# Ten zero products in place of fourteen, a last tile normalised on VectorE, and a new order on every engine

## The chip, the cores and the metric

One NeuronCore of one Trainium2 chip runs the whole kernel. The metric is the device time of one execution in microseconds (us); lower is better. The engines are named as the profile names them: PE (TensorE), DVE (VectorE), ACT (ScalarE), POOL (GpSimd) and SP (SyncE, which here only issues DMAs).

## The reference

`x` is 8 sequences of 512 rows of 256 numbers. A layer of attention with a decaying memory is followed by a gated feed-forward layer on numbers rounded to FP4, each with a layer norm behind it:

```python
# attention: chunked scan, equal to a decaying causal product
v = x @ W_write.T
reads[t] = sum over s < t of gamma**(t-1-s) * (x[t] . x[s-1]) * v[s]      # x[-1] = 0, gamma = sigmoid(decay)
x = layernorm(2 * x + exp(log_alpha) * reads @ W_read.T)
# feed-forward: q(.) rounds blocks of 16 numbers to the FP4 grid with a scale of max|.|/6
h = silu(q(x) @ q(w_gate).T) * (q(x) @ q(w_up).T)                          # 704 wide
x = layernorm(x + q(h) @ q(w_down).T)
```

## The kernel before

Everything stays in SBUF; only the inputs and the output go through HBM. A sequence n is cut into four tiles of 128 rows (k = 4n + t is a tile's number, 0 to 31). fp32 operands are split into a rounded part (`_hi`) and a remainder (`_lo`), and each product is made of three: hi with hi, hi with lo, lo with hi. ACT mostly makes the `_hi` copy, DVE or POOL the remainder.

On PE, for a sequence n: `scores(n, j)` makes row block j of the score matrix (512 - 128j columns, 6 products) and DVE's `decay_scores` multiplies it with the decay mask (`pr`, counted by `pr_ready`); `values(n, u)` multiplies two tiles with the combined weights W_write and W_read (12 products of 256 columns; `v_lo_ready`); `reads(n, u)` multiplies scores and values (9 products for u = 0, 21 for u = 1) and DVE's `x_residual` takes it from PSUM (`z_ready`). The layer norm and the rounding to FP4 go over ACT, DVE and POOL, then `xq_transpose(n, u)` turns two tiles round (4 transposes; `xqT_lo_ready`). For each tile k follow `gate_up(k, b, t, half)` (12 products of 512 columns for half 0, 6 of 384 for half 1), SiLU on ACT, `hidden` on DVE, the rounding of h, `h_transpose(k, t, g)` (4 and 2 transposes; `hT_lo_ready`), `down(k, t)` (17 products of 256 columns) and DVE's `out_residual` (`o_ready`). The layer norm of the output: ACT squares (`out_deviations`), DVE makes -mean and variance (`out_moments`, 128x1), POOL the power -0.5 and then shift = -mean * rstd (`out_rstd`, L417 and L419), ACT the tile itself (`out_layernorm`, L713), and SP stores it.

The weights are combined and rounded at the start by the same engines: `combine` makes W_write.T W_read.T in PSUM, DVE's `scale_comb` multiplies it with alpha, ACT rounds it, DVE's `rest_comb` makes `comb_lo`. `w_maxima` to `w_dequant` round the six blocks of the feed-forward weights, `w_transpose(f)` and `w_subtract(f)` turn them round on PE (`wT_lo_ready`).

Each engine's program is one list of such calls, written out by hand for the start (sequences 0 to 2 or so) and the end, with a loop `body(b)` between for b = 2, 3 and 4 (k = 4b, n = b + 1), which is unrolled. Engines work their list in order and wait on semaphores. PSUM has eight banks of 512 columns: `gu[0]` to `gu[3]` and `bank[0]` to `bank[3]`; several kinds of result share a bank, so most PE calls carry a second wait (`free`, the list in brackets), until DVE or ACT has taken out what the bank held before. Ahead of its real work PE multiplies zeros (L1825), 14 times 512 columns:

```python
pe.wait_ge(zeros_ready, 1)
for _ in range(14):
    nc.tensor.matmul(gu[:, 3, :], zeros[:, 0:P], zeros[:], start=True, stop=True)
```

The loads are issued by SP in the order first half of x transposed (ACT issues the second), weights 0, attention weights, weights 1, x transposed of sequence 1, weights 2, x of sequence 0, weights 3 to 5; later loads wait for the buffer.

Of the kernel before, what the change touches and what calls it, by code (L numbers as in the profile page):

```python
# [37 lines left out]
P = 128  # L38
# [14 lines left out]
def mk_seq_postln_kernel(nc, x_rows, xt_rows, w_attn, w_ffn, scalars, out):  # L53
# [18 lines left out]
    with ExitStack() as ctx:  # L72
# [93 lines left out]
        w_bank = (gu[:, 3, :], bank[0], bank[3], gu[:, 2, :], gu[:, 1, :], gu[:, 0, :], gu[:, 3, :], bank[3], bank[2])  # L166
# [33 lines left out]
        hT_filled, hT_hi_ready, hT_lo_ready = sem("hT_filled"), sem("hT_hi_ready"), sem("hT_lo_ready")  # L200
        down_filled, o_ready, o_dev, o_var, o_rstd_ready, o_shift_ready, out_ready = (
# [52 lines left out]
        def _(sp):  # L254
# [54 lines left out]
            store(11, 3)  # L309
            load_x(7)  # L310
            store(12, 0)
# [18 lines left out]
            store(31, 3)  # L330
# [5 lines left out]
        def _(pool):  # L336
# [89 lines left out]
            p_rest(0, 1)  # L426
            w_dequant(0)
            p_rest(0, 2)
            p_rest(0, 3)
            w_normalise(2)  # L430
            w_dequant(1)
            x_rstd(0, 0)
            p_rest(1, 0)
            p_rest(1, 1)
            w_dequant(2)
            w_normalise(3)
            p_rest(1, 2)
# [1633 lines left out]
```

## Time and profile before

| | us |
|---|---|
| median of 3 runs | 326.65 (326.39 to 327.18) |
| the profiled execution | 326.19 |
| its span, first to last instruction | 324.5 |

A row of a timeline gives the start and the duration in us from the span's start, the engine, the line, the instruction with what it writes and reads, how many were merged (x2), and in brackets how long the engine had been idle before it and what ended that. Durations of PE rows overlap, since products are pipelined: the next starts before the one before has ended.

### The profile page before, as it was taken

How to read it: one execution, taken by the hardware profiler on the slowest of the kernel's cores; microseconds unless marked ns; L12 is line 12 of the kernel's file. 1: busy time of each engine (PE TensorE's matmuls, PEld its weight loads, DVE VectorE, ACT ScalarE, POOL GpSimd, SP SyncE). 2: the span in 40 equal slices, each digit the busy share in tenths (PEclk: the TensorE clock that was granted, in tenths of full speed). 3: DMA queues.
4: the chain of work that ended last, by engine and by line, in shares of the span. 5: the costliest groups of instructions: out<-in, count | busy, mean ns of one | idle time of the engine just before them, and what ended most of it. 6: DMA issues, size and time to landing. Idle time of an engine off the chain costs nothing.

```text
span 324.5 us, 6515 instructions
## 1 busy us (share of the span) xinstructions
PE 314.7 (97%) x2065; PEld 285.2 (88%) x2065; DVE 293.5 (90%) x754; ACT 210.8 (65%) x516; POOL 239.9 (74%) x257
## 2 busy tenths in 40 slices
PE   8999999999999999999999999999999999999993
PEld 3899888979988999899999999899989889999983
DVE  4999898999898999698996989999999999999982
ACT  7378977594915786348926687466657745665774
POOL 1869859857975789956996688687677767569672
PEclk9999999999999999999999999999999999999999
DMA  6821300210010202020010200020000000001002
GB/s 230 295 67 67 128 3 0 68 66 2 1 65 18 82 2 75 24 81 20 32 68 16 83 1 33 2 81 17 18 2 33 18 0 33 19 16 34 33 31 69
DMA packets 8242, 15.69 MB, mean 48 GB/s; under 512 B 1040, under 2 KB 5136, under 8 KB 8208
## 3 DMA queue, kind: packets, MB, share of 16 engines
q1 hardware_dynamic: 7920, 15.01, 13.5%
q8 instruction: 17, 0.28, 0.4%
q10 hardware_dynamic: 288, 0.26, 0.3%
q14 instruction: 17, 0.14, 0.1%
HBM read 11.08 MB, written 4.19 MB: 47 GB/s over the span
## 4 chain that ended last, share of the span: by engine, by line
PE 70%; DVE 18%; issue 6%; ACT 4%; POOL 1%; DVEq 0%; POOLq 0%; ACTq 0%
PE gu L1690 11%; PE gu L1694 11%; PE gu L1691 11%; PE bank L1690 5%; PE bank L1691 5%; PE bank L1694 5%; PE bank L1778 4%; DVE h_y L1071 3%; PE bank L1700 2%; PE bank L1703 2%; PE bank L1704 2%; DVE w_raw L1182 2%; PE bank L1752 2%; PE gu L1825 2%; DVE hqT_lo L1209 2%
## 5 line engine op out<-in xcount | busy, mean ns | idle before, releaser
L410 POOL TENSOR_TENSOR h_q<-h_g,h_ns 128x704 f32<-128x704 f32 x32 | 47.3, 1477 | 39.5 <-DVE h_g L1076 36.0
L1690 PE MATMUL gu<-guT_hi,xqT_hi 128*128 128x512 f32 (+1 forms) x192 | 74.9, 390 | 0.5 <-DVE w_raw L1182 0.5
L1691 PE MATMUL gu<-guT_lo,xqT_hi 128*128 128x512 f32 (+1 forms) x192 | 72.1, 376 | 0.0
L681 ACT ACTIVATE w_raw<-gu 128x512 f32<-128x512 f32 x64 | 29.3, 461 | 47.2 <-PE gu L1694 46.8
L1694 PE MATMUL gu<-guT_hi,xqT_lo 128*128 128x512 f32 (+1 forms) x192 | 56.7, 377 | 0.5 <-DVE xqT_lo L1173 0.5
L403 POOL TENSOR_TENSOR h_n<-w_raw,h_rs 128x704 f32<-128x704 f32 x32 | 49.0, 1531 | 9.3 <-DVE h_rs L1066 8.8
L1690 PEld LDWEIGHTS gu<-guT_hi,xqT_hi 128*128 128x128 f32 x192 | 36.1, 188 | 6.7 <-issue 1.3
L1694 PEld LDWEIGHTS gu<-guT_hi,xqT_lo 128*128 128x128 f32 x192 | 35.6, 188 | 6.7 <-DVE xqT_lo L1173 0.9
L1691 PEld LDWEIGHTS gu<-guT_lo,xqT_hi 128*128 128x128 f32 x192 | 36.2, 188 | 5.2
L1071 DVE SCALAR_TENSOR_TENSOR h_y<-h_sq,h_n 128x704 f32<-128x704 bf16 x34 | 36.3, 1069 | 1.6 <-ACT h_sq L685 1.5
L1182 DVE TENSOR_TENSOR w_raw<-w_raw,gu 128x512 f32<-128x512 f32 x64 | 32.3, 506 | 2.9 <-ACT w_raw L681 2.2
L365 POOL TENSOR_TENSOR pr_lo<-pr,pr_hi 128x512 fp32r<-128x512 f32 (+3 forms) x32 | 29.1, 917 | 3.6 <-ACT pr_hi L645 3.6
L1076 DVE SCALAR_TENSOR_TENSOR h_g<-h_sq,h_y 128x704 f32<-128x704 bf16 x34 | 31.4, 924 | 0.2
L1209 DVE TENSOR_TENSOR hqT_lo<-bank,hqT_hi 128x512 fp32r<-128x512 f32 (+1 forms) x48 | 28.1, 590 | 2.5 <-ACT hqT_hi L701 2.5
L685 ACT ACTIVATE h_sq<-h_n 128x704 bf16<-128x704 f32 x32 | 25.3, 789 | 6.3 <-POOL h_n L403 6.3
L1690 PE MATMUL bank<-dnT_hi,hqT_hi 128*128 128x256 f32 x120 | 29.2, 279 | 0.0
L1691 PE MATMUL bank<-dnT_lo,hqT_hi 128*128 128x256 f32 x120 | 29.2, 279 | 0.0
L417 POOL TENSOR_TENSOR o_rstd<-o_ve,neg_half 128x1 f32<-128x1 f32 x32 | 23.4, 731 | 7.1 <-DVE o_ve L1225 7.1
L701 ACT CAST hqT_hi<-bank 128x512 fp32r<-128x512 f32 (+1 forms) x48 | 24.0, 508 | 7.1 <-PE bank L1778 7.0
L1188 DVE TENSOR_REDUCE h_am<-w_raw 128x44 f32<-128x704 f32 x32 | 27.9, 873 | 0.2
L713 ACT ACTIVATE wq_gu<-wq_gu,o_shift,o_rstd 128x256 f32<-128x256 f32 x32 | 19.1, 598 | 12.0 <-POOL o_shift L419 11.9
L395 POOL TENSOR_TENSOR x_q<-x_g,x_ns 128x512 f32<-128x512 f32 x16 | 18.7, 1167 | 9.0 <-DVE x_g L1076 9.0
(156 smaller groups left out, 941.1 us busy)
## 6 DMA issues: line engine op xcount, KB each, us to landing
xs<-in_x_rows_dram SPq DMA_DIRECT2D x8, 512.0 KB, 3.3
out_dram<-wq_gu SPq DMA_DIRECT2D x32, 128.0 KB, 1.7
x_full<-in_xt_rows_dram SPq DMA_DIRECT2D x7, 512.0 KB, 3.3
w_raw<-in_w_ffn_dram SPq DMA_DIRECT2D x6, 352.0 KB, 5.9
w_pair<-in_w_attn_dram SPq DMA_DIRECT2D x1, 512.0 KB, 5.1
x_full<-in_xt_rows_dram SPq DMA_DIRECT2D x1, 256.0 KB, 2.8
x_full<-in_xt_rows_dram ACTq DMA_DIRECT2D x1, 256.0 KB, 3.4
scal<-in_scalars_dram ACTq DMA_DIRECT2D x1, 1.0 KB, 1.7
```

Of the source, the lines that this page charges most:

```text
L365: nc.gpsimd.tensor_tensor(pr_lo[:, c], pr[:, c], pr_hi[:, c].bitcast(F32), ALU.subtract).then_inc(pr_lo_ready, 1)
L403: nc.gpsimd.tensor_tensor(blocks(h_n[:, p, :]), blocks(h[:, p, :]), per_block(h_rs[:, p, :], HB), ALU.mult).then_inc(h_norm, 1)
L410: nc.gpsimd.tensor_tensor(blocks(h_q[:, p, 0:I]), blocks(h_g[:, p, :]), per_block(h_ns[:, p, :], HB), ALU.mult).then_inc(h_quant, 1)
L681: nc.scalar.activation(silu[:, p, part[half]], gate_of[half], ACT.Silu).then_inc(silu_ready, 1)
L1071: nc.vector.scalar_tensor_tensor(y, sq, MAGIC_C, v, ALU.add, ALU.add).then_inc(magic_sem, 1)
L1076: nc.vector.scalar_tensor_tensor(g, sq, MAGIC_C, y, ALU.add, ALU.subtract).then_inc(grid_sem, 1)
L1182: nc.vector.tensor_tensor(h[:, p, c], silu[:, p, c], up_of[half], ALU.mult).then_inc(h_ready, 1)
L1188: nc.vector.tensor_reduce(h_am[:, p, :, 0:4], blocks(h[:, p, :]), AX.X, ALU.max, apply_absolute_value=True).then_inc(h_amax, 1)
L1209: nc.vector.tensor_tensor(hqT_lo[:, p, c], h_bank[t][g][:, 0:c.stop - c.start], hqT_hi[:, p, c].bitcast(F32), ALU.subtract).then_inc(hT_lo ...
L1690: nc.tensor.matmul(dst, lh, rh, start=(first and i == 0), stop=False)
L1691: nc.tensor.matmul(dst, lh, rl, start=False, stop=False)
L1694: last = nc.tensor.matmul(dst, ll, rh, start=False, stop=(end and i == len(terms) - 1))
```

## The change

- PE multiplies zeros 10 times in place of 14.
- The last tile (k = 31) is normalised by one DVE instruction, (z - mean) * rstd, in place of POOL's shift and ACT's `out_layernorm`. POOL still makes the power; SP's last store waits for the new semaphore `o_last`.
- The lists of all engines are in another order, the loop's too, and the PSUM banks are assigned otherwise, with other `free` waits. Apart from the two points above the calls of each engine are the same ones.
- On SP `store(12, 0)` stands ahead of `load_x(7)`.

```diff
-        v_bank, xq_bank = (bank[2], bank[1]), (bank[1], bank[3])
-        s_bank, r_bank = (gu[:, 3, :], bank[0], bank[3], gu[:, 3, :]), (bank[2], bank[1])
-        h_bank = ((bank[1], bank[0]), (bank[1], bank[0]), (bank[2], gu[:, 3, :]), (bank[3], gu[:, 3, :]))
-        d_bank = (bank[3], bank[0], bank[2], gu[:, 3, :])
+        v_bank, xq_bank = (bank[0], bank[1]), (bank[1], bank[3])
+        s_bank, r_bank = (bank[1], bank[3], bank[2], gu[:, 3, :]), (bank[0], gu[:, 3, :])
+        h_bank = ((bank[1], gu[:, 3, :]), (bank[1], bank[0]), (bank[2], bank[3]), (bank[2], bank[3]))
+        d_bank = (gu[:, 3, :], gu[:, 3, :], bank[0], bank[2])
...
+            store(12, 0)
             load_x(7)
-            store(12, 0)
...
-            store(31, 3)
+            sp.wait_ge(o_last, 1)
+            sp.dma_start(out_rows[31], o_out[:, 3, :]).then_inc(stored[3], 16)
...
-            out_rstd(31, 1)
+            pool.wait_ge(o_var, 32)
+            nc.gpsimd.tensor_tensor(o_rstd[:, 1:2], o_ve[:, 1:2], neg_half[:, 0:1], ALU.pow).then_inc(o_rstd_ready, 1)
...
+            def out_finish(k, b, t):
+                p = t % 2
+                c = slice(p, p + 1)
+                dve.wait_ge(o_var, k + 1)
+                dve.wait_ge(o_rstd_ready, k + 1)
+                dve.wait_ge(stored[t], b * 16 + 16)
+                nc.vector.tensor_scalar(o_out[:, t, :], o_z[:, p, :], o_nm[:, c], o_rstd[:, c], ALU.add,
+                                        ALU.mult).then_inc(o_last, 1)
```

The opening of DVE's list after `w_reciprocals(1)`, before and after:

```python
# before
scale_comb(); decay_scores(0, 0); decay_scores(0, 1); rest_comb(); w_magic_add(0); w_to_grid(0); w_maxima(2); v_rest(0, 0)
# after
decay_scores(0, 0); scale_comb(); w_magic_add(0); rest_comb(); decay_scores(0, 1); decay_scores(0, 2); w_to_grid(0)
```

PE's list, the stretches that the prediction speaks of, as before (-) and after (+):

```diff
-            w_transpose(5, [])
-            w_subtract(4)
+            w_transpose(5, [])
+            scores(2, 2, [(wT_lo_ready, 2)])
+            scores(2, 3, [(z_ready, 4)])
+            w_subtract(4)
...
-            xq_transpose(1, 0, [(z_ready, 6)])
-            scores(3, 1, [(pr_ready, 10)])
-            w_subtract(8)
-            gate_up(4, 1, 0, 0)
+            xq_transpose(1, 0, [(pr_ready, 13)])
+            scores(3, 1, [(wT_lo_ready, 9)])
+            values(3, 0, [(wT_lo_ready, 8)])
+            h_transpose(0, 0, 0, [(xqT_lo_ready, 3)])
+            h_transpose(0, 0, 1, [(z_ready, 6)])
+            gate_up(4, 1, 0, 0)
...
             # in body(b)
-                xq_transpose(n - 1, 0, [(v_lo_ready, 2 * n + 2)])
-                scores(n + 1, 1, [(o_ready, 4 * n - 10)])
-                down(k - 6, 2, [(z_ready, 2 * n + 1)])
-                reads(n, 1, [(xqT_lo_ready, 2 * n - 1)])
-                h_transpose(k - 5, 3, 1, [(pr_ready, k + 9)])
-                gate_up(k, b, 0, 0)
+                reads(n, 1, [(o_ready, 4 * n - 10)])
+                xq_transpose(n - 1, 0, [(pr_ready, 4 * n + 5)])
+                values(n + 1, 0, [(o_ready, 4 * n - 9)])
+                h_transpose(k - 5, 3, 1, [(hT_lo_ready, 2 * k - 10)])
+                gate_up(k, b, 0, 0)
+                h_transpose(k - 4, 0, 0, [(xqT_lo_ready, 2 * n - 1)])
+                down(k - 5, 3, [(hT_lo_ready, 2 * k - 9)])
+                scores(n + 1, 1, [(hT_lo_ready, 8 * n - 16)])
+                scores(n + 1, 2, [(o_ready, 4 * n - 8)])
...
+                scores(n + 1, 3, [(hT_lo_ready, 8 * n - 14)])
+                h_transpose(k - 2, 2, 0, [(pr_ready, k + 11)])
+                gate_up(k + 1, b, 1, 1)
+                down(k - 4, 0, [(pr_ready, k + 12)])
...
             # after the loop
-            scores(7, 0, [(hT_lo_ready, 30)])
-            gate_up(19, 4, 3, 1)
-            h_transpose(15, 3, 1, [(pr_ready, 29)])
+            scores(n + 2, 0, [(v_lo_ready, 2 * n + 4)])   # end of the loop's body, scores(7, 0) in its last pass
+            down(14, 2, [(z_ready, 13)])
+            reads(6, 1, [(o_ready, 14)])
+            h_transpose(15, 3, 1, [(hT_lo_ready, 30)])
+            h_transpose(16, 0, 0, [(pr_ready, 29)])
```

## Rows read from the trace of the kernel before

**Rows 1.** The page's busy times: us, share of the span, instructions:

```profile
PE 314.7 (97%) x2065; PEld 285.2 (88%) x2065; DVE 293.5 (90%) x754; ACT 210.8 (65%) x516; POOL 239.9 (74%) x257
```

**Rows 2.** Windows: width, then PE, PEld, DVE, ACT, POOL busy us, clock, DMA:

```profile
12.79:102.00 89.21, 87.37 (x564) 78.62 (x564) 82.34 (x196) 62.27 (x146) 72.05 (x70) 1.00 0.16 55
102.00:212.00 110.00, 110.00 (x742) 102.07 (x741) 100.93 (x268) 69.19 (x180) 84.88 (x89) 1.00 0.11 38
212.00:310.00 98.00, 97.05 (x647) 89.18 (x647) 95.61 (x243) 62.59 (x157) 70.78 (x75) 1.00 0.08 25
```

**Rows 3.** PE's waits, first and last of nine rows (us, times, longest):

```profile
PE gu L1825 <- DVE zeros L1042: 1.3, 1, 1.3
...
PE gu L1802 <- DVE pr L1112: 0.2, 1, 0.2
```

**Rows 4.** Timeline of the opening: start, us, engine, line, instruction:

```profile
1.25 5.91 PE L1825 MATMUL gu<-zeros 128*128 128x512 bf16 x14 [1.25 <-DVE zeros L1042]
...
2.23 0.42 DVE L1048 TENSOR_SCALAR dist<-dist 128x512 f32<-128x512 f32 x1
...
4.70 1.12 ACT L631 CAST xT_hi<-x_full 128x512 fp32r<-128x512 f32 x2
...
5.33 1.29 DVE L1104 TENSOR_TENSOR xT_lo<-x_full,xT_hi 128x512 fp32r<-128x512 f32 x2 [1.69 <-ACT xT_hi L631]
...
6.82 0.81 PE L1700 MATMUL gu<-xT_hi 128*128 128x512 f32 x2
...
7.47 0.40 PE L1703 MATMUL gu<-xT_lo,xT_hi 128*128 128x512 f32 x1
...
7.71 0.39 PE L1704 MATMUL gu<-xT_hi,xT_lo 128*128 128x512 f32 x1
...
8.39 1.89 PE L1819 MATMUL bank<-w_pair 128*128 128x256 f32 x8
...
12.79 0.39 PE L1690 MATMUL bank<-comb_hi,xT_hi 128*128 128x256 f32 x1
```

**Rows 5.** DVE's timeline from 9 to 13 us:

```profile
10.32 0.75 DVE L1232 TENSOR_SCALAR comb<-bank,scal 128x512 f32<-128x512 f32 x1 [0.54 <-PE bank L1819]
...
12.05 0.68 DVE L1237 TENSOR_TENSOR comb_lo<-comb,comb_hi 128x512 fp32r<-128x512 f32 x1
12.65 0.88 DVE L1071 SCALAR_TENSOR_TENSOR h_y<-gu,h_n 128x704 f32<-128x704 f32 x1
```

**Rows 6.** Timeline of PE ahead of and after its stops:

```profile
27.34 0.52 PE L1802 MATMUL gu<-ident,wq_gu 128*128 128x128 f32 x3 [0.18 <-DVE pr L1112]
...
35.14 0.46 PE L1810 MATMUL gu<-guT_hi,neg_ident 128*128 128x384 f32 x1 [0.34 <-ACT guT_hi L612]
...
69.14 0.74 PE L1694 MATMUL gu<-guT_hi,xqT_lo 128*128 128x512 f32 x2 [0.50 <-DVE xqT_lo L1173]
...
101.53 0.59 PE L1700 MATMUL bank<-v_hi,pr_hi 128*128 128x256 f32 x3 [0.57 <-DVE xqT_lo L1173]
...
211.61 0.51 PE L1694 MATMUL gu<-guT_hi,xqT_lo 128*128 128x384 f32 x2
212.49 0.41 PE L1778 MATMUL gu<-ident,h_q 128*128 128x128 f32 x2 [0.37 <-DVE pr L1112]
...
221.27 0.39 PE L1690 MATMUL gu<-guT_hi,xqT_hi 128*128 128x512 f32 x1
```

**Rows 7.** Timeline of the end:

```profile
318.93 0.28 PE L1792 MATMUL gu<-dnT_hi,hqT_lo 128*128 128x256 f32 x1
319.43 0.42 DVE L1218 SCALAR_TENSOR_TENSOR wq_gu<-gu,x 128x256 f32<-128x256 f32 x1 [1.62 <-ACT wq_gu L713]
...
320.83 0.54 POOL L417 TENSOR_TENSOR o_rstd<-o_ve,neg_half 128x1 f32<-128x1 f32 x1
...
321.44 0.19 POOL L419 TENSOR_TENSOR o_shift<-o_nm,o_rstd 128x1 f32<-128x1 f32 x1
321.67 0.60 ACT L713 ACTIVATE wq_gu<-wq_gu,o_shift,o_rstd 128x256 f32<-128x256 f32 x1 [0.16 <-POOL o_shift L419]
```

More of the change, by code:

```diff
@@ L1839, in _ @@
             scores(1, 1, [(pr_ready, 2)])
-            reads(0, 1, [(v_lo_ready, 2)])
             values(1, 0, [(z_ready, 1)])
             scores(1, 2, [(pr_ready, 3)])
-            scores(1, 3, [(pr_ready, 5)])
-            values(1, 1, [(z_ready, 2)])
-            w_transpose(0, [(pr_ready, 8)])
-            w_transpose(1, [(pr_ready, 6)])
-            w_transpose(2, [(pr_ready, 7)])
+            w_transpose(0, [(pr_ready, 6)])
+            values(1, 1, [(pr_ready, 5)])
+            w_subtract(0)
@@ L1863, in _ @@
             pe.wait_ge(wT_lo_ready, 6)
             gate_up(0, 0, 0, 0)
+            gate_up(0, 0, 0, 1)
             values(2, 1, [(xqT_lo_ready, 1)])
-            scores(2, 2, [(wT_lo_ready, 3)])
-            gate_up(0, 0, 0, 1)
             gate_up(1, 0, 1, 0)
-            scores(2, 3, [(pr_ready, 9)])
-            xq_transpose(0, 1, [(pr_ready, 11)])
+            xq_transpose(0, 1, [(pr_ready, 10)])
             gate_up(1, 0, 1, 1)
+            reads(2, 0, [(v_lo_ready, 5)])
             gate_up(2, 0, 2, 0)
+            w_transpose(6, [(pr_ready, 11)])
@@ L1873, in _ @@
+            w_transpose(7, [(z_ready, 5)])
             gate_up(2, 0, 2, 1)
[L1874 to L1875 removed]
+            scores(3, 0, [(v_lo_ready, 6)])
+            w_subtract(6)
+            w_transpose(8, [(xqT_lo_ready, 2)])
+            reads(2, 1, [(pr_ready, 12)])
+            w_subtract(7)
+            w_subtract(8)
             gate_up(3, 0, 3, 0)
[L1877 to L1879 removed]
@@ L1906, in body @@
+            gate_up(6, 1, 2, 0)
+            h_transpose(2, 2, 0, [(pr_ready, 15)])
+            h_transpose(2, 2, 1, [(xqT_lo_ready, 4)])
+            down(1, 1, [(pr_ready, 16)])
+            reads(3, 0, [(hT_lo_ready, 4)])
+            gate_up(6, 1, 2, 1)
+            h_transpose(3, 3, 0, [(hT_lo_ready, 5)])
+            gate_up(7, 1, 3, 0)
+            scores(4, 0, [(v_lo_ready, 8)])
             def body(b):
                 k, n = b * 4, b + 1
-                gate_up(k - 2, b - 1, 2, 0)
@@ new lines, in body @@
+                values(n + 1, 1, [(hT_lo_ready, 8 * n - 13)])
+                xq_transpose(n - 1, 1, [(pr_ready, 4 * n + 6)])
+                scores(n + 1, 3, [(hT_lo_ready, 8 * n - 14)])
+                h_transpose(k - 2, 2, 0, [(pr_ready, k + 11)])
+                gate_up(k + 1, b, 1, 1)
+                down(k - 4, 0, [(pr_ready, k + 12)])
+                gate_up(k + 2, b, 2, 0)
+                reads(n + 1, 0, [(hT_lo_ready, 8 * n - 12)])
+                h_transpose(k - 2, 2, 1, [(xqT_lo_ready, 2 * n)])
@@ L1955, in _ @@
+            gate_up(19, 4, 3, 1)
+            down(15, 3, [(hT_lo_ready, 31)])
+            h_transpose(16, 0, 1, [(z_ready, 14)])
             xq_transpose(5, 0, [(hT_lo_ready, 33)])
-            h_transpose(16, 0, 1, [(pr_ready, 30)])
-            values(7, 0, [(o_ready, 15)])
+            scores(7, 1, [(hT_lo_ready, 32)])
             gate_up(20, 5, 0, 0)
-            reads(7, 0, [(v_lo_ready, 15)])
+            xq_transpose(5, 1, [(pr_ready, 30)])
+            scores(7, 2, [(o_ready, 16)])
@@ L1960, in _ @@
+            gate_up(20, 5, 0, 1)
             h_transpose(17, 1, 0, [(xqT_lo_ready, 11)])
-            gate_up(20, 5, 0, 1)
-            h_transpose(17, 1, 1, [(hT_lo_ready, 34)])
-            down(16, 0, [(pr_ready, 31)])
+            h_transpose(17, 1, 1, [(v_lo_ready, 15)])
             gate_up(21, 5, 1, 0)
-            xq_transpose(5, 1, [(o_ready, 17)])
+            down(16, 0, [(hT_lo_ready, 34)])
+            values(7, 1, [(hT_lo_ready, 35)])
+            h_transpose(18, 2, 0, [(pr_ready, 31)])
@@ L1966, in _ @@
+            scores(7, 3, [(o_ready, 17)])
+            reads(7, 0, [(hT_lo_ready, 36)])
             gate_up(21, 5, 1, 1)
-            scores(7, 3, [(o_ready, 16)])
-            values(7, 1, [(hT_lo_ready, 35)])
-            h_transpose(18, 2, 0, [(z_ready, 15)])
             gate_up(22, 5, 2, 0)
-            h_transpose(18, 2, 1, [(pr_ready, 32)])
             gate_up(22, 5, 2, 1)
-            down(17, 1, [(hT_lo_ready, 36)])
+            h_transpose(18, 2, 1, [(xqT_lo_ready, 12)])
+            down(17, 1, [(pr_ready, 32)])
```

1214 lines of the change are left out of this document (591 added, 623 removed).

## The prediction

> **What bounds the kernel now.** I read the page's busy times first, then the windows, the list of PE's waits, the timeline of the opening and of the end, and the rows ahead of PE's stops. PE is busy 97% of the span and DVE 90% [rows 1]; the reader is to see that both queues are nearly full, so work on one is cheap only where it waits for the other. By windows [rows 2] the middle is PE's: from 102 to 212 us PE has no idle time at all while DVE is busy 100.93 of 110. From 212 to 310 both are full (97.05 and 95.61 of 98). In these three windows PE idles 1.84, 0 and 0.95 us, 2.8 together.
>
> The idle time understates a stop. In [rows 6] two 384-column products from 211.61 are shown 0.51 long, but such products start 0.176 apart (the 0.235 of a 512-column one, below, by 384 / 512), so PE could go on at 211.96; it did at 212.49. The stop was 0.53 and the idle time shown 0.37, 0.16 less. The list of waits has nine rows with ten waits, of which one is the start [rows 3]; nine stops with 0.16 each added make PE's recoverable time 2.8 + 1.4 = 4.2 us. That is the most that a new order can give back; what PE multiplies does not change (each engine's calls are the same but for those named below).
>
> **The opening, 14 zero products to 10.** They start at 1.25 and the first real product follows at 6.82 [rows 4]. A product of 512 columns takes 512 / 1.2 GHz = 0.427 at TensorE's lower level, and 13 of them are 5.55 of the 5.57 between (two of the fourteen start almost together), so four fewer are 1.71: PE is free at 5.11. The first scores need both casts of x, which end at 4.70 + 1.12 = 5.82, and their last four products need the remainder, at 5.33 + 1.29 = 6.62 [rows 4]. So PE's real work can start 0.95 us earlier, and after the remainder some 0.6 us earlier.
>
> Whether that counts is decided by DVE. The products with the combined weights, which start at 12.79 [rows 4], wait for comb_lo, which ended at 12.05 + 0.68 = 12.73 [rows 5]. DVE stands idle for 0.54 ahead of scale_comb at 10.32, from 9.78, for the combine [rows 5]. In the new order it does decay_scores(0, 0) in that gap (0.60 of queue time: durations here exceed the spacing by 0.08, as 12.05 to 12.65 shows), then scale_comb 0.75 - 0.08 = 0.67, w_magic_add(0) 0.88 and rest_comb 0.60, with 0.08 at the end: 9.78 + 0.60 + 0.67 + 0.88 + 0.60 + 0.08 = 12.61, against 12.73 [rows 5]. PE, earlier by 0.6, waits for DVE there. The four zero products give **-0.1 us**; if magic_add slipped behind, it would be -0.9, so the bounds are 0 and -0.9.
>
> The zero products also set TensorE's clock. That spacing of 0.427 is the 1.2 GHz level, and those from 7.47 to 7.71 on are spaced 0.235, the 2.4 GHz level [rows 4]; the second level came after PE had been fed from 1.25 to about 6.8 without a gap. The change leaves a gap of 0.76 us (5.11 to 5.87) in that stretch. In the Trainium skill, "TensorE: Matmul & The Clock Gate", section "What's actually happening", the slow level is the default and sustained activity releases it, at a moment that varies from run to run. By that rule a later release is possible here; no row of before shows a gap in that stretch, and the price is worked out as a rival below.
>
> **The end.** After the last product (318.93) come the residual at 319.43, the square, the moments, the power at 320.83 for 0.54, then the shift on POOL at 321.44 and the normalisation on ACT from 321.67 for 0.60, to 322.27 [rows 7]; the store follows. The change removes shift and ACT step for this tile: DVE's one instruction can start 0.07 after the power's end (as the shift did), at 321.44. Its duration isn't shown for 128x256 with two columns as operands; a 128x512 one with constants is 0.42 [rows 4], and the 128x256 residual, which reads two tensors, is 0.42 [rows 7]. That is the upper bound, half of the first (0.21) the lower; I take 0.32, nearer to the tensor_scalar. End at 321.76 in place of 322.27: **-0.5 us** (-0.4 to -0.6). The store behind it is as before. DVE has nothing queued behind it.
>
> **The order: stops that get cover.** Cover is PE work between the producer of what is waited for and the waiting block, from the code and spacings of 0.235, 0.176 and 0.12 for 512, 384 and 256 columns and 0.11 for a transpose. (1) At 69.14 gate_up(4, 1, 0, 0) waits for xqT_lo, idle 0.50, so 0.66 [rows 6]; its transposes lie 1.3 us ahead (scores(3, 1) and a w_subtract); new, 3.1 (scores(3, 1), values(3, 0) and h_transpose(0)). (2) At 101.53 reads(3, 1) waits for bank 1 that xq_transpose(2, 0) filled: 0.57 + 0.16 = 0.73. In the new assignment reads use gu[3], freed by a down some 9 us earlier. (3) At 212.49 h_transpose(15, 3, 1) waits for scores(7, 0) to be taken out of gu[3], with only 1.05 of cover: 0.53; new, it is h_transpose(16, 0, 0) with 4.7. (4) At 35.14 w_subtract(4) follows w_transpose(5) at once, 0.34 + 0.16 = 0.50; new, scores(2, 2) and (2, 3) lie between, 1.4. Together **-2.4 us**. If these run into DVE again just behind, 0; so 0 to -2.4 for the four.
>
> **The order: covers that get short.** In the loop, scores(n+1, 2) now waits for out_residual(k-5) in bank 2 with only scores(n+1, 1) between: 6 x 0.176 = 1.05. After a last product at 318.93 the residual ended at 319.43 + 0.42 = 319.85, 0.92 later [rows 7]; the cover is 0.12 + 1.05 = 1.17. With DVE free that is no stop; with DVE busy, the same 1.05 of cover at 212.49 cost 0.53 [rows 6]. And down(k-4) waits for decay_scores(n+1, 3) with a transpose and half a gate_up between, 1.5; the nearest row is 27.34, cover 1.42, idle 0.18, a stop of 0.34 [rows 6]. Before, the shortest such cover in the loop was 2.4. I take 0.25 and 0.15, three times each, 1.2 us, and 0.1 for scores(2, 1) at 1.65: **+1.3 us**, between 0 and 3 x (0.53 + 0.34) = 2.6, or more if DVE lags. The fresh gate_up(k, b, 0, 0) gets 1.6 of cover for its xqT_lo where it had 5.8; gate_up(20, 5, 0, 0) had the same 1.6 and started at 221.27 with no idle time [rows 6], so I add nothing; without a free DVE it would cost 0.66 as at 69.14. On SP only store(12) and load_x(7) change places; the load then also waits for tile 12's normalisation, which the old order asked for next on that queue anyway, so nothing. POOL and ACT queues are reshuffled too, but POOL is busy 70.78 of 98 and ACT 62.59 of 98 [rows 2], and I cost them at nothing; if a POOL dequantisation comes late, its transposes stop PE.
>
> **Sum.** -0.1 - 0.5 - 2.4 + 1.3 = -1.7. The profiled execution took 326.19 (its span 324.5), so 324.5; the median of the three runs, 326.65, is 0.46 above it. Forecast: 325.0.
>
> **Rivals.** *The loop's short covers stop PE every time.* DVE is a queue in order, 92% busy there [rows 2]; if it is behind at each of the six places, each costs like the largest stop seen, 0.73: 6 x 0.73 = 4.4 in place of 1.2, so 328.2, slower than before. It decides once the six average 0.64 ((327.63 - 325.0) / 6 + 0.2). Against it speaks that a cover of 1.17 exceeds the 0.92 needed. *The stops only move.* With both queues full from 212 on [rows 2], PE saved 0.5 here is lost to DVE there: only opening and end remain, 326.65 - 0.6 = 326.0, no change that can be told. *The clock comes late.* Ten zero products do not do what fourteen did: six scores products at 0.427 from 5.87 end at 8.43; the combine's 1.89 [rows 4] stays or doubles, so it ends between 10.3 and 12.2, and 0.67 + 0.88 + 0.68 more on DVE put comb_lo between 12.6 and 14.5, in the middle 0.8 later than before and 0.9 later than forecast: 325.9. *Most stops vanish.* All 4.2 us and 0.6: 326.65 - 4.8 = 321.8, if the order fits the real durations well; the room is there in [rows 2], mostly before 102 us.
>
> **How the numbers follow.** Chances: forecast 0.42 (own range 323.9 to 326.0), most stops vanish 0.20, stops only move 0.18, clock late 0.05, loop stops 0.15. The range from 321.9 to 327.9 leaves out the far ends of the first and last rival. 0.3% is 0.98 us, about what this measurement can tell from no change: below 325.67 lie the forecast's larger part (0.37) and the vanishing case, 0.57; between, 0.28; above 327.63, 0.15.
>
> **What would show it.** PE's first real product near 5.9 and the combined weights' first near 12.7; last normalisation on DVE, 0.2 to 0.4 long; no PE wait on xqT_lo near 69 and 101, none on pr near 212; in the loop's three passes, stops ahead of scores(n+1, 2) and down(k-4) of 0 to 0.5 us. Wrong would make it: PE idle time between 102 and 212 above 2 us, products at 0.427 spacing after 7 us, or PE waits on POOL's h_q.

## The result and the profile after

The kernel after takes 327.97 us (median of 8 runs, 327.31 to 328.72); the kernel before took 326.49 beside it (8 runs). The ratio is 1.0048, interval 1.0036 to 1.0061: slower, by 1.5 us. The forecast was 325.0 and its range ended at 327.9. The profiled execution's span went from 324.46 to 325.64. The spans of all runs lie further apart than the times: their median is 326.25 in the kernel after (8 runs, 325.6 to 327.0) and 324.1 in the kernel before (63 runs beside the experiments, 323.9 to 324.9), 2.1 us. What a time holds outside its span is 1.7 to 2.1 us in the new order and 1.7 to 2.9 in the old; why is open.

The page's busy times of the kernel after, beside [rows 1]:

```profile
PE 314.3 (97%) x2061; PEld 285.1 (88%) x2061; DVE 297.7 (91%) x755; ACT 213.0 (65%) x515; POOL 241.5 (74%) x256
```

The same windows as [rows 2], and the end (width, then PE, PEld, DVE, ACT, POOL busy):

```profile
12.79:102.00 89.21, 87.46 (x578) 79.90 (x577) 85.84 (x203) 63.59 (x149) 73.13 (x69) 1.00 0.16 55
102.00:212.00 110.00, 109.31 (x731) 100.68 (x730) 99.91 (x262) 70.69 (x178) 85.39 (x91) 1.00 0.13 39
212.00:310.00 98.00, 96.37 (x636) 87.89 (x634) 95.53 (x241) 61.70 (x154) 71.03 (x74) 1.00 0.07 24
310.00:325.60 15.60, 10.12 (x82) 9.42 (x80) 7.96 (x30) 8.98 (x24) 6.82 (x14) 0.97 0.16 52
```

The middle has idle time on PE that it did not have (0.69 of 110) and from 212 on it is 1.63 where it was 0.95. DVE is 4.2 us busier in total although only one instruction of 0.41 came to it; why is read below, under what the runs showed of the hardware. PE's waits, of which [rows 3] had nine rows and here are thirteen (us, times, longest):

```profile
PE gu L1703 <- DVE w_raw L1184: 1.0, 4, 0.3
PE gu L1707 <- DVE xqT_lo L1175: 0.6, 1, 0.6
PE gu L1716 <- DVE v_lo L1120: 0.5, 1, 0.5
PE bank L1713 <- DVE wq_gu L1220: 0.5, 1, 0.5
PE gu L1801 <- DVE wq_gu L1220: 0.4, 1, 0.4
...
PE bank L1823 <- ACT guT_hi L615: 0.4, 1, 0.4
...
PE bank L1707 <- DVE hqT_lo L1211: 0.2, 1, 0.2
```

And where they lie, as rows of PE's timeline (compare [rows 6]):

```profile
26.94 0.50 PE L1823 MATMUL bank<-guT_hi,neg_ident 128*128 128x512 f32 x1 [0.42 <-ACT guT_hi L615]
...
31.45 0.39 PE L1716 MATMUL gu<-v_lo,pr_hi 128*128 128x256 f32 x1 [0.54 <-DVE v_lo L1120]
...
39.94 0.66 PE L1765 MATMUL bank<-ident,x_q 128*128 128x128 f32 x4 [0.44 <-POOL x_q L397]
...
112.36 0.50 PE L1703 MATMUL gu<-guT_hi,xqT_hi 128*128 128x512 f32 x1 [0.23 <-DVE w_raw L1184]
...
217.90 0.84 PE L1707 MATMUL bank<-dnT_hi,hqT_lo 128*128 128x256 f32 x5 [0.25 <-DVE hqT_lo L1211]
...
222.10 0.74 PE L1707 MATMUL gu<-guT_hi,xqT_lo 128*128 128x512 f32 x2 [0.61 <-DVE xqT_lo L1175]
...
225.15 0.48 PE L1713 MATMUL bank<-xT_hi 128*128 128x256 f32 x2 [0.46 <-DVE wq_gu L1220]
...
243.58 0.50 PE L1703 MATMUL gu<-guT_hi,xqT_hi 128*128 128x512 f32 x1 [0.32 <-DVE w_raw L1184]
...
313.64 0.35 PE L1801 MATMUL gu<-dnT_hi,hqT_hi 128*128 128x256 f32 x1 [0.45 <-DVE wq_gu L1220]
```

A stop is idle time plus about 0.16, as the prediction worked out. The three at 217.90, 222.10 and 225.15 are 0.41, 0.77 and 0.63. The row at 112.36 stands for one in each pass of the loop (also 150.00 and 187.66, 0.39 each).

**Where the time went.** PE's start of a product, less the regular spacings of all real products ahead of it (0.2335 for 512 columns, 0.1755, 0.1178 for 256, and so on, 300.1 in all), is what PE has lost so far. Taken at the same kind of mark in both traces, and set beside the forecast's terms:

| stretch | lost before | lost after | change | forecast |
|---|---|---|---|---|
| to the products with the combined weights | 7.42 | 7.11 | -0.31 | -0.1 |
| to the loop's first block (84.6, 95.5) | 4.84 | 4.62 | -0.22 | -1.06 |
| the loop (to 199, 208.5) | 2.22 | 2.98 | +0.76 | +0.47 |
| to 212.4, 213 | 0.62 | 0.02 | -0.60 | -0.53 |
| to 228, 230 | 0.55 | 2.41 | **+1.86** | 0 |
| to the last product (318.93, 320.41) | 3.18 | 3.17 | -0.01 | 0 |
| last product to the span's end | 5.53 | 5.23 | -0.30 | -0.5 |

The sum is +1.18, the difference of the two profiled spans, against -1.7. It sets one execution beside one other, and the first row is within what varies by itself: the products with the combined weights start between 12.10 and 13.04 in the five traces of the old order and between 12.42 and 12.98 in the nine of the new.

### The profile page after: what moved, and what is told of

It reads as the page before. It is cut to its first block, busy times and chain, and to the rows that moved or that the text cites. A ratio compares the mean times of both kernels' runs of the same rounds, so it can differ in the third digit from the quotient of the medians.

```text
span 325.6 us, 6506 instructions
## 1 busy us (share of the span) xinstructions
PE 314.3 (97%) x2061; PEld 285.1 (88%) x2061; DVE 297.7 (91%) x755; ACT 213.0 (65%) x515; POOL 241.5 (74%) x256
## 4 chain that ended last, share of the span: by engine, by line
PE 71%; DVE 18%; issue 5%; ACT 3%; POOL 2%; ACTq 0%; DVEq 0%; POOLq 0%
PE gu L1703 14%; PE gu L1707 14%; PE gu L1704 14%; PE bank L1791 5%; PE bank L1703 3%; PE bank L1704 3%; PE bank L1707 3%; DVE h_y L1073 2%; PE bank L1765 2%; DVE pr L1114 2%; PE bank L1713 2%; PE gu L1716 2%; PE gu L1717 2%; PE bank L1717 2%; PE bank L1716 2%
## 5 line engine op out<-in xcount | busy, mean ns | idle before, releaser
L412 POOL TENSOR_TENSOR h_q<-h_g,h_ns 128x704 f32<-128x704 f32 x32 | 48.3, 1509 | 46.5 <-DVE h_g L1078 46.2
L405 POOL TENSOR_TENSOR h_n<-w_raw,h_rs 128x704 f32<-128x704 f32 x32 | 47.8, 1495 | 7.2 <-DVE h_rs L1068 7.2
L704 ACT CAST hqT_hi<-bank 128x512 fp32r<-128x512 f32 (+1 forms) x56 | 26.9, 489 | 11.5 <-PE bank L1791 8.8
L1211 DVE TENSOR_TENSOR hqT_lo<-bank,hqT_hi 128x512 fp32r<-128x512 f32 (+1 forms) x56 | 31.1, 560 | 2.2 <-ACT hqT_hi L704 2.2
L367 POOL TENSOR_TENSOR pr_lo<-pr,pr_hi 128x512 fp32r<-128x512 f32 (+3 forms) x32 | 30.4, 954 | 1.0 <-ACT pr_hi L648 1.0
L1078 DVE SCALAR_TENSOR_TENSOR h_g<-h_sq,h_y 128x704 f32<-128x704 bf16 x34 | 30.4, 896 | 0.0
L1791 PE MATMUL bank<-ident,h_q 128*128 128x128 f32 x176 | 27.2, 273 | 0.0
L419 POOL TENSOR_TENSOR o_rstd<-o_ve,neg_half 128x1 f32<-128x1 f32 x31 | 22.4, 723 | 3.9 <-DVE o_ve L1227 3.8
L708 ACT ACTIVATE o_off<-wq_gu,o_sum 128x256 bf16<-128x256 f32 x32 | 16.1, 504 | 12.6 <-DVE wq_gu L1220 12.4
L1791 PEld LDWEIGHTS bank<-ident,h_q 128*128 128x128 f32 x176 | 21.0, 140 | 2.8 <-issue 0.2
```

Of the source, the lines that this page charges most:

```text
L367: nc.gpsimd.tensor_tensor(pr_lo[:, c], pr[:, c], pr_hi[:, c].bitcast(F32), ALU.subtract).then_inc(pr_lo_ready, 1)
L405: nc.gpsimd.tensor_tensor(blocks(h_n[:, p, :]), blocks(h[:, p, :]), per_block(h_rs[:, p, :], HB), ALU.mult).then_inc(h_norm, 1)
L412: nc.gpsimd.tensor_tensor(blocks(h_q[:, p, 0:I]), blocks(h_g[:, p, :]), per_block(h_ns[:, p, :], HB), ALU.mult).then_inc(h_quant, 1)
L1078: nc.vector.scalar_tensor_tensor(g, sq, MAGIC_C, y, ALU.add, ALU.subtract).then_inc(grid_sem, 1)
L1211: nc.vector.tensor_tensor(hqT_lo[:, p, c], h_bank[t][g][:, 0:c.stop - c.start], hqT_hi[:, p, c].bitcast(F32), ALU.subtract).then_inc(hT_lo ...
L1791: last = nc.tensor.transpose(h_bank[t][g][:, at - h_part[g].start:at - h_part[g].start + P], h_q[:, t % 2, at:at + P], ident[:])
```

## The experiments

Twelve kernels ran. All ratios are to the kernel before. The opening differs by up to 0.9 us between kernels whose instructions are the same up to there (below), so half a microsecond between two kernels is read from the stretch concerned and not from the times alone.

**What holds DVE (after, and before, with one-column moments).** In the loop of the kernel after, DVE's timeline has a two-element instruction that takes 1.27 us, and POOL's has one that ends with it:

```profile
109.04 1.27 DVE L1146 TENSOR_SCALAR z_nm<-z_sum 128x2 f32<-128x2 f32 x1
110.22 0.16 DVE L1147 TENSOR_SCALAR z_ve<-z_ssq 128x2 f32<-128x2 f32 x1
```

```profile
108.89 1.39 POOL L405 TENSOR_TENSOR h_n<-w_raw,h_rs 128x704 f32<-128x704 f32 x1
```

109.04 + 1.27 = 110.31, POOL's end is 108.89 + 1.39 = 110.28. It is so in every pass (146.68 behind 146.53), and `w_raw`, for which PE stops at 112.36, stands five instructions behind. The same layer's output moments, one column each, show no such case in any of 32. So the edit splits the instruction, in the kernel after (`e1_columns`) and alike in the kernel before (`e4_before_columns`):

```diff
-                nc.vector.tensor_scalar(z_nm[:, c], z_sum[:, c], -1.0 / D, None, ALU.mult)
+                for i in (2 * u, 2 * u + 1):
+                    nc.vector.tensor_scalar(z_nm[:, i:i + 1], z_sum[:, i:i + 1], -1.0 / D, None, ALU.mult)
```

(and `z_ve` likewise).

> The changed kernel, with DVE's two-column moments (z_nm and z_ve, 128x2) written as two one-column instructions each. In the changed kernel z_nm took 1.26 us in each pass of the loop (at 109.04, 146.68 and 184.34) and ended 0.02 us after POOL's h_normalise ended, and its 16 instances took 10.2 us where 0.16 each would be 2.5; the one-column o_nm never took over 0.2. Theory A (DVE is held by POOL in this form): the holds go, the stop of 0.39 us ahead of gate_up(k+1, b, 1, 0) goes in all three passes, and the time falls by 1.2 to 2.5 us against the changed kernel, to about 326.2. Theory B (the order alone: hidden(k, 0, 0) stands behind decay_scores(n+1, 1), which waits for PE): the stops stay, and the time stays within 0.5 us of the changed kernel, 328.0. Theory C (POOL's port holds whatever DVE runs next): the hold moves to the next instruction of DVE, and the time stays.

> The kernel before with the moments in one-column instructions. There z_nm and z_ve took 10.3 us in all, 5.3 above 0.16 each, but in the loop PE stopped nowhere for them. Theory A: DVE is free for 4 us more; PE stops of some 0.5 to 1.5 us after 200 us shrink, time 326.5 - 0.5 to 1.5. Theory B: no change, within 0.3 us. A loss of up to 0.5 us is possible, since the new form has 32 more instructions on DVE with 0.06 us each.

Measured: 324.25 (ratio 0.9927, interval 0.9913 to 0.9942) and 322.48 (0.9868, 0.9849 to 0.9887). Both gain more than expected, 3.7 and 4.2 us. The instruction's durations (minimum, median, maximum in ns), in the kernel after and then with the edit:

```profile
L1146 DVE TENSOR_SCALAR z_nm<-z_sum x16: 126/555/1357, 22.5 to 256.8; 128x2 f32<-128x2 f32 x16
```

```profile
L1147 DVE TENSOR_SCALAR z_nm<-z_sum x32: 96/144/154, 23.0 to 254.1; 128x1 f32<-128x1 f32 x32
```

and in the kernel before:

```profile
L1144 DVE TENSOR_SCALAR z_nm<-z_sum x16: 98/170/1123, 21.6 to 252.4; 128x2 f32<-128x2 f32 x16
```

The hold on this instruction is real and costs both kernels some 4 us; the loop's stops on `w_raw` go. But it is not what the change cost: without it the new order is still 1.8 us behind the old one, as with it (1.5). By the accounting of the table the edited pair has lost 12.51 and 12.14 up to the loop's end, and behind it 5.06 and 2.97: nearly the whole difference lies behind the loop.

**The loop's stop by order (`e2_hidden_first`).** DVE's list in the loop, the kernel after:

```diff
-                decay_scores(n + 1, 1)
                 hidden(k, 0, 0)
+                decay_scores(n + 1, 1)
```

> The changed kernel with one exchange in DVE's loop: hidden(k, 0, 0) ahead of decay_scores(n+1, 1). Theory B (order): the three stops of 0.39 us ahead of gate_up(k+1, b, 1, 0) go, time 1.2 us below the changed kernel, and they go although z_nm still takes 1.26. Theory A (hold by POOL): decay_scores takes 0.46 of DVE's time, so the exchange alone also removes the stop of 0.39, but z_nm stays long and what is behind it comes as late as before; only 0.5 to 1.2 us. If neither, the stops reappear at scores(n+1, 3) or at the second half of gate_up and the time stays at 328.0.

Measured: 327.1, ratio 1.0011 (1.0000 to 1.0021). PE's idle time between 102 and 212 is gone:

```profile
102.00:212.00 110.00, 110.00 (x737) 101.55 (x736) 101.27 (x263) 71.27 (x179) 86.15 (x91) 1.00 0.13 39
```

So these three stops, 1.2 us, were on the path and were worth 0.9 in the medians and 1.2 in the ratios. They go although `z_nm` still takes 1.26 (at 109.46), as theory B has it. Since they also go when the hold does (`e1_columns`), they need both: the held instruction and the mask product ahead of `hidden(k, 0, 0)`.

**The zero products (`e3_zeros14`)**, the kernel after with 14 of them.

```diff
-            for _ in range(10):
+            for _ in range(14):
```

> The changed kernel with 14 zero products again. PE started its products with the combined weights at 12.47 in the changed kernel and at 12.79 before. If the four zero products are hidden by DVE's work on comb_lo, as predicted, the time changes by 0 to 0.3 us. If they count in full, it is 1.7 us slower, 329.7. If the earlier gap makes the clock come late and this costs, it gets faster by up to 1 us.

Measured: 327.84, ratio 1.0033 (1.0020 to 1.0046), below the kernel after by 0.1 in the medians and by 0.5 in the ratios, whose intervals overlap. Its products with the combined weights start at 12.51, against 12.47:

```profile
1.25 5.72 PE L1838 MATMUL gu<-zeros 128*128 128x512 bf16 x14 [1.25 <-DVE zeros L1044]
...
12.51 0.39 PE L1703 MATMUL bank<-comb_hi,xT_hi 128*128 128x256 f32 x1
```

In the new order the number of zero products is worth nothing: DVE sets that start, as forecast. No run has ten zero products in the old order, where DVE stands idle for 0.54 ahead of `scale_comb`, so what they are worth there is open.

**The end (`e5_old_end`: the kernel after with the last tile done as before; `e6_before_end`: the kernel before with the new last tile).**

```diff
-            out_finish(31, 7, 3)            # DVE
+            out_rstd(31, 1)                 # POOL
+            out_layernorm(31, 7, 3)         # ACT
```

> The changed kernel with the last tile normalised as before (shift on POOL, ACT's out_layernorm). From the last product's start to the end of the span the changed kernel took 5.2 us (320.41 to 325.6) and the kernel before 5.5 (318.93 to 324.5). If the new end is worth what was predicted, this is 0.3 to 0.5 us slower than the changed kernel, about 328.4; if it is worth nothing, 328.0.

> The kernel before with only the last tile's normalisation moved to DVE. DVE's instruction took 0.41 us in the changed kernel where I took 0.32, so 0.4 less than before: 326.1. If POOL's queue ahead of the last power is what counts, 0.0 to 0.2 less.

Measured: 328.0 (1.0048, 1.0032 to 1.0064) and 326.34 (1.0001, 0.9988 to 1.0015). In time neither can be told from its counterpart. The traces show it all the same: from the last product's start to the span's end it is 5.42 to 5.53 us in the four kernels with the old end and 5.14 to 5.26 in the ten with the new one. So the new end is worth 0.3 in the traces, and too little to be seen in the times.

**Repairing the covers behind the loop (`e9_three_covers`; `e8_bank29` has the last of its edits alone).** On top of `e2_hidden_first`, `xq_rest(5, 0)` goes ahead of `h_magic_add(18, 0)`, for the stop at 222.10, and tile 29's product fills bank 1 instead of `gu[3]`, for the stop at 313.64.

```diff
-            down(29, 1, [(o_ready, 29)])          # into gu[3]
+            down(29, 1, [(hT_lo_ready, 59)])      # into bank[1]
...
+            xq_rest(5, 0)
             h_magic_add(18, 0)
             x_reciprocals(6, 0)
-            xq_rest(5, 0)
```

> The changed kernel, its moments left as they are (two columns), with three repairs of its order: hidden(k, 0, 0) ahead of decay_scores(n+1, 1) in DVE's loop (three stops of 0.39), down(29) in bank 1 in place of gu[3], which down(28) had just filled (stop of 0.61 at 313.64), and xq_rest(5, 0) ahead of a h_magic_add (stop of 0.77 at 222.10). If these stops are why the order is slower, the sum is 1.2 + 0.6 + 0.8 = 2.6 us: 325.4, about 1 us faster than before. If stops only move to the next wait, the first is worth the 1.2 that it was alone and the other two nothing: 326.8 or more.

> The kernel after with down(29) filling bank 1 in place of gu[3], so that it need not wait for out_residual(28) to take the product of tile 28 out of the same bank (the stop of 0.61 at 313.64). Theory 'this stop is on the path to the end': 0.3 to 0.6 less, 327.4 to 327.7, which is at the edge of what can be told. Rival 'the stop only moves, since the products behind wait for DVE's residuals and remainders of the same tiles anyway': within 0.2 of the kernel after, with a new stop of some 0.3 to 0.6 between 314 and 317 us.

Measured: 326.75 (1.0009, 0.9998 to 1.0021), in the ratio nothing beyond `e2_hidden_first` (0.35 less in the medians); and 327.76 (1.0045, 1.0032 to 1.0058), nothing beyond the kernel after. PE's stops in the first, in the two places:

```profile
217.49 0.85 PE L1710 MATMUL bank<-dnT_hi,hqT_lo 128*128 128x256 f32 x5 [0.24 <-DVE hqT_lo L1214]
...
223.20 0.63 PE L1768 MATMUL bank<-ident,x_q 128*128 128x128 f32 x4 [0.25 <-DVE pr L1117]
...
224.62 0.48 PE L1716 MATMUL bank<-xT_hi 128*128 128x256 f32 x2 [0.80 <-DVE wq_gu L1223]
```

```profile
314.21 0.84 PE L1710 MATMUL bank<-dnT_hi,hqT_lo 128*128 128x256 f32 x5 [0.20 <-DVE hqT_lo L1214]
315.35 0.88 PE L1794 MATMUL bank<-ident,h_q 128*128 128x128 f32 x6 [0.18 <-POOL h_q L415]
```

0.77 and 0.63 became 0.40 and 0.96; 0.61 became 0.36 and 0.34. Here stops only move: putting one DVE call earlier makes the calls behind it late by about the same amount, and PE meets them next.

**Less work for DVE behind the loop (`e11_light_after`, `e12_light_before`, `e13_light_columns`).** DVE has next to no idle time in the kernel after from 213 to 225 us. Parts of it, at 213.65 and from 217 on:

```profile
213.65 1.52 DVE L1078 SCALAR_TENSOR_TENSOR x_g<-x_sq,x_y 128x512 f32<-128x512 bf16 x1
...
217.44 1.01 DVE L1211 TENSOR_TENSOR hqT_lo<-bank,hqT_hi 128x256 fp32r<-128x256 f32 x2
218.37 2.88 DVE L1073 SCALAR_TENSOR_TENSOR h_y<-h_sq,h_n 128x704 f32<-128x704 bf16 x2
221.16 0.34 DVE L1068 RECIPROCAL x_rs<-x_sc 128x32 f32<-128x32 f32 x1
221.43 0.62 DVE L1175 TENSOR_TENSOR xqT_lo<-bank,xqT_hi 128x512 fp32r<-128x512 f32 x1
...
223.50 1.10 DVE L1146 TENSOR_SCALAR z_nm<-z_sum 128x2 f32<-128x2 f32 x1
...
224.58 0.41 DVE L1220 SCALAR_TENSOR_TENSOR wq_gu<-bank,x 128x256 f32<-128x256 f32 x1
```

with POOL beside it:

```profile
213.55 1.06 POOL L397 TENSOR_TENSOR x_q<-x_g,x_ns 128x512 f32<-128x512 f32 x1
...
218.77 1.72 POOL L397 TENSOR_TENSOR x_q<-x_g,x_ns 128x512 f32<-128x512 f32 x1
...
223.19 1.39 POOL L412 TENSOR_TENSOR h_q<-h_g,h_ns 128x704 f32<-128x704 f32 x1 [2.69 <-DVE h_g L1078]
```

`x_g` is 1.52 where it takes 0.68 unheld. The pair of `h_y` is 2.88 where two take 1.68 unheld (0.88, the second starting 0.80 behind the first), and delays `xqT_lo` (the stop at 222.10); `z_nm`, held to POOL's end at 224.58 and 1.10 long in place of 0.16, delays the residual (the stop at 225.15). Together DVE is held for 3.0 us in this stretch. In the kernel before two instructions between 212.4 and 227.9 are held, 0.66 and 0.28 us beyond their 0.88, 0.9 together:

```profile
215.67 1.54 DVE L1076 SCALAR_TENSOR_TENSOR h_g<-h_sq,h_y 128x704 f32<-128x704 bf16 x1
...
223.93 1.16 DVE L1071 SCALAR_TENSOR_TENSOR h_y<-h_sq,h_n 128x704 f32<-128x704 bf16 x1
```

The difference, 2.0, is as large as the 1.86 that the new order loses more here.

```diff
-                magic_add(h_y[:, p, :], h_sq[:, p, :], h_n[:, p, :], h_square, h_magic, k + 1)
+                c = slice(0, 352) if k in (17, 18) else slice(0, I)
+                magic_add(h_y[:, p, c], h_sq[:, p, c], h_n[:, p, c], h_square, h_magic, k + 1)
```

(`h_to_grid` likewise.)

> The kernel after, in which DVE's two rounding steps (magic_add and to_grid) of tiles 17 and 18 go over 352 of 704 columns; the second half of those two tiles keeps what an earlier tile left there. Nothing else is changed. These four instructions are 0.88 long where nothing holds them, so DVE has some 4 x 0.37 = 1.5 us less to do between 213 and 224 us. Theory 'DVE is full behind the loop' (in the kernel after it has no idle time at all from 213 to 225 us, and PE stops there at 217.90, 222.10 and 225.15 for what is late on DVE, 1.8 us together): the three stops shrink to under 0.6 together and the time falls by 1.0 to 2.0, to 326.0 to 327.0. Rival 'a chain of latencies, not the amount of DVE's work, sets these stops': the time falls by under 0.4.

> The kernel before with the same four instructions of tiles 17 and 18 cut to 352 of 704 columns (the second half keeps what an earlier tile left). Theory 'DVE is full behind the loop, in the new order alone': here DVE is idle several times between 212 and 224 us and PE has a single stop, of 0.53 at 212.49, ahead of most of these instructions, so the gain is under 0.5. Rival 'DVE's work bounds both orders in the same degree there': the gain is as large as in the kernel after, 1.0 or more.

> The kernel after with the moments of x made in one-column instructions (324.25 when it ran alone) and the four shortened instructions of tiles 17 and 18 on top. Theory 'DVE is full behind the loop': the stops that were left between 210 and 220 us (1.35 us) mostly go, and the time falls by 0.8 to 1.5 more, to 322.7 to 323.5, near the 322.5 that the kernel before with the one-column instructions reached. Rival 'once nothing is held, DVE's amount of work no longer counts there': 323.9 or more.

Measured: 326.72 (1.0013, 1.0001 to 1.0025), 325.33 (0.9973, 0.9960 to 0.9986) and 323.53 (0.9917, 0.9904 to 0.9931). The third is 0.7 below `e1_columns` in the medians and 0.3 in the ratios: at or under the lower end of what was expected, so little is left for the amount of work once `z_nm` is not held. For the pair of the two orders, by the times alone, the rival holds: the kernel before gained 1.06 where under 0.5 was expected, nearly the 1.25 of the kernel after. The traces place the gains differently. A window of the same stretch in four kernels, the kernel after, then light, then the kernel before, then light:

```profile
213.00:230.00 17.00, 15.68 (x100) 13.83 (x100) 16.89 (x41) 10.87 (x28) 11.26 (x14) 1.00 0.11 40
```

```profile
213.00:229.00 16.00, 15.66 (x100) 13.90 (x99) 15.80 (x42) 10.65 (x27) 11.08 (x14) 1.00 0.13 42
```

```profile
212.40:228.00 15.60, 15.44 (x113) 14.72 (x114) 14.93 (x42) 9.89 (x26) 12.41 (x15) 1.00 0.14 48
```

```profile
212.40:227.50 15.10, 15.10 (x114) 14.52 (x113) 13.89 (x41) 10.27 (x27) 12.21 (x14) 1.00 0.12 45
```

PE's idle time goes from 1.32 to 0.34 in the new order, and from 0.16 to 0 in the old; lost time (as in the table) from 2.41 to 1.27, and from 0.55 to 0.25. `xqT_lo` starts at 220.50, where it started at 221.43, and the stops at 222.10 and 225.15 are gone; the one at 217.90, which lies ahead of the shortened instructions, stays (0.40, at 217.71). The new order's gain of 1.25 thus lies nearly whole in this stretch (1.14). Of the old order's 1.06, 0.30 lies there and some 0.6 ahead of 12.1 us, long before the shortened instructions: its products with the combined weights started at 12.10, where they had at 12.79 [rows 4]. The medians of the spans side with the traces: 1.35 in the new order (326.25 to 324.9), 0.55 in the old (324.0 to 323.45). So that DVE's lateness sets two of PE's three stops behind the loop in the new order is shown; that less work helps the new order more than the old is seen in traces and spans and not in the times.

**Both improvements in the old order (`e10_before_columns_end`)**: one-column moments and the new end.

> The kernel before with the one-column moments (4.2 us faster by themselves) and the new end: 322.5 - 0.4 = 322.1. If the end's saving and the moments' overlap, 322.5.

Measured: 322.67 (0.9891, 0.9872 to 0.9911), the same as `e4_before_columns` alone. These two are the fastest of all, and neither has the new order.

## Why the prediction was wrong

- **The zero products: right in the mechanism.** PE's first real product started at 5.97 (forecast near 5.9) and the combined weights' first at 12.47 (12.7), with 14 zero products at 12.51. DVE did its mask product in the gap ahead of `scale_comb`, as worked out. The rival of the late clock fell: the remainder products at 7.30, 7.54 and 7.77 are 0.235 apart, the 2.4 GHz level, and `comb` starts at 10.29, not later than [rows 5]. The first real products, 0.56 and 0.43 apart, were still at the lower level. The Trainium skill's rule ("TensorE: Matmul & The Clock Gate", "What's actually happening"), by which a later release was possible, cost nothing here. That the term came out (-0.3 against -0.1) is no more than the opening varies by itself. One reading of rows was wrong, without effect on the sum: no two of the fourteen zero products start together (0.40 to 0.43 apart); it is the first real product that starts 0.05 behind the last of them.

```profile
5.97 1.19 PE L1713 MATMUL bank<-xT_hi 128*128 128x512 f32 x2 [0.27 <-ACT xT_hi L634]
...
12.47 0.39 PE L1703 MATMUL bank<-comb_hi,xT_hi 128*128 128x256 f32 x1 [0.22 <-DVE comb_lo L1249]
```

- **The end: the mechanism right, the size a little off.** From the last product to the span's end it is 5.23 after 5.53, so -0.3 and not -0.5. Up to the end of the normalisation the gain is as forecast, 3.33 to 2.90 (-0.4), although DVE's instruction takes 0.41, the upper bound and not the 0.32 taken. POOL's shift of tile 30 stands ahead of the last power, as it did in the kernel before (at 320.68), and costs little: `o_ve` is ready at 321.96 + 0.14 = 322.10, and the power starts at 322.26, 0.16 later, where it had been 0.08. The term at fault is "the store behind it is as before": from the store's issue to the span's end it is 2.28 to 2.30 in the ten kernels with the new end and 2.17 in the four with the old one, 0.1 more; why is open.

```profile
322.12 0.19 POOL L421 TENSOR_TENSOR o_shift<-o_nm,o_rstd 128x1 f32<-128x1 f32 x1
322.26 0.54 POOL L585 TENSOR_TENSOR o_rstd<-o_ve,neg_half 128x1 f32<-128x1 f32 x1
```

```profile
322.90 0.41 DVE L1237 TENSOR_SCALAR wq_gu<-wq_gu,o_nm,o_rstd 128x256 f32<-128x256 f32 x1 [0.80 <-DVE o_ve L1227]
```

- **Stops that get cover: all four went, and ahead of the loop others took their place.** There is no stop at 35.14's, 69.14's, 101.53's or 212.49's place. But ahead of the loop 1.16 of it should have been gained and 0.22 was: new stops at 26.94 (0.58, the first `w_subtract` waiting for ACT), 31.45 (0.70, `reads(1, 1)` waiting for `v_lo`) and 39.94 (0.60, an `xq_transpose` waiting for POOL's `x_q`) stand against it. The prediction covered single stops and did not follow the list behind each.
- **Covers that get short: the size near by luck, the place wrong.** Neither `scores(n+1, 2)` nor `down(k-4)` stopped PE in the loop. What did was `hidden(k, 0, 0)`, late on DVE behind a held `z_nm` and a mask product: three stops of 0.39, 1.2 together, where 1.2 had been put for others. The loop cost +0.76 against +0.47; the middle had 0.69 of idle time, below the 2 us that would have told against the forecast.
- **Nothing for the stretch behind the loop: the step that failed.** The sum prices short covers for the loop's three passes and one stop at 212.49, and behind 213 nothing. For the fresh `gate_up` it says "I add nothing", on one row, `gate_up(20, 5, 0, 0)` at 221.27 with 1.6 of cover and no idle time [rows 6]. In the loop that came out: with 1.6 of cover no pass stops there. But the call of that row has only `scores(7, 1)`, 1.05, as its cover in the new order, which was not looked at, and it stops for 0.77 at 222.10, because DVE reaches `xqT_lo` late. That is the price named (0.66, "without a free DVE") and not put into the sum. Likewise `scores(7, 2)`, the call behind the loop that answers to `scores(n+1, 2)`, waits for `out_residual(15)` and stops for 0.63 at 225.15, although some 5 us of PE's work lie between; the prediction counted this wait three times, in the loop, where it cost nothing. With 0.41 at 217.90 the three are 1.8 us, and from 213 to 230 the new order loses 1.86 more than the old, more than the 1.5 by which the times differ. What the runs show in place of the prediction's account is that a cover's length did not decide there, but when DVE came to the result: it was held for 3.0 us in this stretch, against 0.9 before. It came nearest to the rival of stops that only move, with a sign: they moved to where DVE is full, and grew.
- **POOL costed at nothing.** It stops PE only once (39.94), but it holds DVE, which does. With the hold on `z_nm` taken away both kernels gain about alike, so the price of that hold in the change itself is small; its price in either kernel, about 4 us, was in none of the forecast's cases. The holds on `x_g` and `h_y` behind the loop, 2.0 us in the new order, stay in `e1_columns` (1.51 and 2.87 long, at 211.45 and 216.17), and with them the stops that answer to 217.90 and 222.10.

What stays open is how much of the loss behind the loop each part is worth. Holds are a part of it: the traces give their size, but no run takes those on `x_g` and `h_y` away. DVE's amount of work is another (`e13_light_columns` loses 4.37 there, `e1_columns` 5.06, `e4_before_columns` 2.97); about 1.4 us of the difference is left. No run exchanges the list of one engine alone between the two orders, nor separates the new assignment of the banks from the new order.

## What to carry to other kernels

A cover was worth its length here only where the engine that produces what is waited for came to it in time; where its window is full, ask what its queue holds at that moment, and expect a repaired stop to come back at its next late result. Before reordering such a kernel, look for instructions far above the usual duration of their form: here splitting two two-element instructions was worth more than twice what the whole new order cost. And a comparison of two rows with the same cover holds only for the order in which they were read.

## What the runs showed of the hardware

**POOL holds DVE for whole instructions.** DVE's two-column `tensor_scalar` from and to SBUF takes 0.10 to 0.17 us free, and in the kernel after nine of the fifteen `z_nm` that started while POOL was at work ended late, each 0.02 to 0.03 us after POOL's instruction (109.04 above). Of the other six four started within 0.13 us of POOL's end, and two (45.51 and 206.58) ended before it, beside POOL's power. (In the kernel before one more, at 65.91, was not held: it started 0.05 us behind POOL's `h_q` and took 0.10.) The one-column form was not held in any of 29 such cases, 24 of which ended while POOL was still at work.

`h_y`, `x_y`, `h_g` and `x_g`, where they read two SBUF tensors, are held too and end about 0.75 us (704 columns) or 0.55 (512) after POOL's instruction: such is the pair at 218.37, which ends at 221.25 with POOL done at 220.49. Two kinds of overlap did not hold in the kernel after: the `h_y` of the weights, which read one PSUM tensor (the one at 15.52 took 0.88 and ended 0.19 before POOL's instruction), and instructions beside POOL's power (three `h_y`, 0.88 long each, ended 0.60 after it). Counted over the whole span as what each DVE instruction took beyond the usual duration of its form, DVE is held for 22.3 us in the kernel after and 17.5 in the kernel before; the 4.8 between them are about the 4.2 us by which it is busier.

The Trainium skill has the lock ("SBUF — State Buffer", "SBUF: two separate sides"): VectorE and GpSimd share a port pair, whichever takes it first has it for the whole instruction, and VectorE needs it with two SBUF inputs or in a mode that reads one tensor through both ports. The trace agrees for two SBUF inputs, and differs beside POOL's power, as said. "VectorE: DVE Perf Modes", "Mode 2×_2P — use both read ports for one tensor", in the Trainium skill, describes that mode for a `tensor_scalar`: each port streams one half of the tensor. The trace agrees: two columns are held, and one column, which has no halves, is not. That this mode is what the two-column form ran in is concluded from that and not shown by itself.

**The opening varies by itself, for two reasons that the traces show.** The products with the combined weights started at 12.79 in the kernel before and at 12.10 in `e12_light_before`, with the same instructions ahead of them. In the first the zero products are 0.40 to 0.43 apart to the last, TensorE's level of 1.2 GHz, and the row is 5.91 long [rows 4]; in the second they are 0.216 apart from the ninth on, the level of 2.4 GHz. PE was busy with them from 1.25 in both:

```profile
1.25 4.75 PE L1827 MATMUL gu<-zeros 128*128 128x512 bf16 x14 [1.25 <-DVE zeros L1042]
```

So the first real product started at 5.96 where it had at 6.82, and `scale_comb`, for which DVE had been idle, at 9.69 in place of 10.32. The kernel after (12.47) and `e8_bank29` (12.85) differ by something else: both start their real products at 5.97, but the second block of feed-forward weights landed at 8.11 in the one and at 8.48 in the other, where DVE was idle for it:

```profile
8.51 0.89 DVE L1087 TENSOR_REDUCE h_am<-w_raw 128x44 f32<-128x704 f32 x1 [0.28 <-DMA w_raw<-in_w_ffn_dram]
```
